# Logits in eight 64x32 tiles over two banks, spaced gathers and another order of the end: an image kernel on one Trainium2 core

## The reference, cut to what matters

```
x = x + conv_ref(ln_c(x))              # LayerNorm over channels, GroupNorm in 8 groups,
                                       # 1x1 conv, relu, 1x1 conv
t = to_tokens(x)                       # 16384 tokens of 64 values per image
t = t + ffn_ref(ln_t(t))

def ffn_ref(x):                        # 32 experts, each takes its 8 best tokens
    logits = einsum('bsd,ed->bse', x, gate_w) + gate_b
    probs  = softmax(logits, axis=1)   # over the tokens of an image
    vals, idx = top_k(probs.transpose(0, 2, 1), 8)
    gathered = take_along_axis(x, flat_idx)
    pooled = einsum('bked,bke->bed', gathered, vals)
    h = gelu([pooled, 1] @ weight1[e]) # 64 -> 256
    out = [h, 1] @ weight2[e]          # 256 -> 64
    outputs.at[flat_idx].add(out * vals)
```

## Time and profile before

| what | value |
|---|---|
| three runs | 659.89, 661.95, 662.16 us, median 661.95 |
| profiled execution | 660.21 us, its span 658.5 us |
| PE busy | 546.5 us, 83% |
| DVE busy | 488.9 us, 74% |
| ACT busy | 429.1 us, 65% |
| POOL busy | 186.4 us, 28% |
| images in the middle | 65.0 us each |
| last image and end | from 502.75 us on |

### The profile page before, as it was taken

The page is one execution under the profiler, slowest core; times in us unless marked ns, Lnnn a source line. Parts: engine busy times, 40 slices in busy tenths (PEclk is TensorE's granted clock), DMA queues, the critical chain, the costliest instruction groups (busy, mean ns, idle before and its releaser), DMA issues.

```text
span 658.5 us, 14319 instructions
## 1 busy us (share of the span) xinstructions
PE 546.5 (83%) x5838; PEld 278.4 (42%) x5838; DVE 488.9 (74%) x955; ACT 429.1 (65%) x603; POOL 186.4 (28%) x110
## 2 busy tenths in 40 slices
PE   3669989998989898989898989898879849768693
PEld 1234444443444344444444444344434314247563
DVE  5575565889788978897889789978886838697501
ACT  2454778678967896888688867887788525543110
POOL 1008252207120712070208020802070540010612
PEclk9856999999999999999999999999989968796555
DMA  8950246533644364436444543454112524310000
GB/s 197 198 122 26 80 135 171 137 112 109 172 122 121 109 179 108 127 113 177 113 114 119 170 128 100 127 162 128 42 58 99 166 83 129 102 65 1 20 10 8
DMA packets 26753, 73.40 MB, mean 111 GB/s; under 512 B 4152, under 2 KB 4152, under 8 KB 22592
## 3 DMA queue, kind: packets, MB, share of 16 engines
q1 hardware_dynamic: 25664, 71.44, 39.5%
q0 software_dynamic: 1024, 1.05, 0.6%
HBM read 38.40 MB, written 34.08 MB: 110 GB/s over the span
## 4 chain that ended last, share of the span: by engine, by line
PE 41%; DVE 29%; ACT 13%; issue 12%; another core or an unknown queue 2%; DMA 2%; POOL 0%; SPq 0%; ACTq 0%; POOLq 0%; DVEq 0%
PE st L364 10%; ACT junk L737 7%; DVE xs L878 6%; PE cv L375 6%; PE tl L392 5%; PE cv L383 5%; PE bc L485 5%; DVE us L868 5%; DVE lg L866 3%; DVE top_i L965 2%; ACT tok L702 2%; DVE us L870 2%; DVE cnd L960 2%; ACT hid L697 2%
## 5 line engine op out<-in xcount | busy, mean ns | idle before, releaser
L1283 POOL TENSOR_TENSOR xs<-xs,us 128x1024 f32<-128x1024 f32 x64 | 151.1, 2376 | 365.9 <-DVE xs L878 173.1
L878 DVE SCALAR_TENSOR_TENSOR xs<-cv,vecs,xs 128x1024 f32<-128x1024 f32 x64 | 82.1, 1282 | 59.5 <-PE cv L383 49.0
L697 ACT ACTIVATE hid<-cv,b1n 128x1024 f32<-128x1024 f32 x64 | 71.2, 1113 | 42.5 <-PE cv L375 42.1
L730 ACT ACTIVATE sqc<-us 128x1024 f32<-128x1024 f32 x64 | 67.5, 1055 | 44.0 <-DVE us L868 43.3
L868 DVE TENSOR_TENSOR us<-xs,bc 128x1024 f32<-128x1024 f32 x60 | 72.9, 1216 | 19.2 <-PE bc L485 18.8
L392 PEld LDWEIGHTS tl<-ident,xs 128*128 128x128 f32 x512 | 63.8, 195 | 54.6 <-issue 54.4
L485 PE MATMUL bc<-rstd_s,spread 32*128 32x256 f32 x368 | 48.4, 340 | 41.3 <-DVE gsum L870 20.3
L364 PE MATMUL st<-xs,stat_w 128*32 128x256 f32 x1024 | 73.7, 409 | 10.6 <-DMA xs<-in_x 9.0
L737 ACT ACTIVATE junk<-us 128x1024 bf16<-128x1024 f32 x64 | 67.3, 1051 | 22.8 <-DVE gsum L870 22.1
L870 DVE CUSTOM_DVE_ANT_0 us<-us,bc 128x1024 f32<-128x1024 f32 x60 | 72.9, 1215 | 11.2 <-PE bc L485 10.0
L401 PE MATMUL tl<-xs,gcen 128*32 128x256 f32 x1024 | 71.6, 390 | 7.8 <-ACT tok L702 6.8
(11 more groups left out here) (184 smaller groups left out, 654.4 us busy)
## 6 DMA issues: line engine op xcount, KB each, us to landing
xs<-in_x SPq DMA_DIRECT2D x64, 512.0 KB, 6.9
out_rows<-tok SPq DMA_DIRECT2D x64, 512.0 KB
us<-in_e_w SPq DMA_DIRECT2D x8, 260.0 KB
xs<-in_e_w SPq DMA_DIRECT2D x8, 256.0 KB
sqc<-out_rows,idx_all POOLq DMA_INDIRECT x16
out_rows<-sqc,idx_all POOLq DMA_INDIRECT x16, 2.1
vecs<-in_b SPq DMA_DIRECT2D x4, 0.2 KB, 13.7
gate_bias<-in_gate_b SPq DMA_DIRECT2D x4, 0.1 KB, 12.1
```

Source lines behind the costliest of these rows:

```text
L697: nc.scalar.activation(hid[:], cv[:], ACT.Relu, bias=b1n[:, par:par + 1]).then_inc(h_done, 1)
L878: nc.vector.scalar_tensor_tensor(out=xu, in0=cv[:], scalar=vecs[:, 3:4], in1=xu, op0=ALU.add, op1=ALU.add).then_inc(x1_done, 1)
L1283: nc.gpsimd.tensor_tensor(xu, xu, su, ALU.add).then_inc(s_done, 1)
```

## The change

1. `logits` uses eight tiles of 64 input rows by 32 output columns. The two halves of the pixels go to two banks, `lgp` and `pt`, 256 columns in each, so the zero half of the weights is no longer multiplied. `logits_copy` reads 256 columns of both banks.
2. The L and E spreads use four products of 64x128 from a new constant `spread2`, which VectorE builds at the start by 32 small operations. The scaling takes a whole piece of 1024 contiguous columns and needs two units of logits and no others; `top_values` waits for its own piece only.
3. The ring has 5 pieces in place of 6; buffers that lay in the sixth are put elsewhere.
4. `candidates` has two more operations on 128x32, since the places inside a piece are laid out otherwise.
5. The token norm of images 0 to 5 runs in steps 5, 6 and 7, and its ScalarE part one step later.
6. Before gathers 0 to 5 GpSimd waits for the last image's x1 of 2, 3 and 4 units and its relu of 4, 5 and 6 units, in turn.
7. In the end, M comes right behind `experts_turn(0)`, all top-8 work stands ahead of VectorE's copies of the turn, and `add_rows` is split: the first half stands ahead of pass 1's `experts_in`, the second behind its `experts_up`. Pass 1's token norm stands ahead of the first `result_rows` and `equal_pixels(3)`.

```diff
-RING = 6
+RING = 5
-DIAGS_AT, PAIR_AT, NORM_AT = (1, 2, 3), (2, 4, 5), (4, 5, 6)
+DIAGS_AT, PAIR_AT, NORM_AT = (1, 2, 3), (2, 4, 5), (5, 6, 7)
...
-        h_banks, add_banks = (st1[:], pt, pd, pc), (st1[:], pc)
+        h_banks, add_banks = (st1[:], pt, pd, pc), (lgp, st2[:])
...
-                            c, col = 2 * sub + h, UN * u + CH * sl + SUB * sub
-                            mm = pe.matmul(lgp[NE * c:NE * c + NE, SUB * sl:SUB * sl + SUB], gcen[:, NE * h:NE * h + NE],
-                                           xs[par][:, col:col + SUB], start=True, stop=True)
+                            c, col, r = 2 * sl + sub, UN * u + CH * sl + SUB * sub, slice(C * h, C * h + C)
+                            mm = pe.matmul(lg_banks[h][NE * c:NE * c + NE, 0:SUB], gcen[r, NE * h:NE * h + NE],
+                                           xs[par][r, col:col + SUB], start=True, stop=True)
...
+                if kind in ("L", "E"):
+                    for h in range(2):
+                        for w in range(2):
+                            r, col = slice(C * w, C * w + C), P * (2 * k + h)
+                            mm = pe.matmul(bc[:, CH * w + SUB * h:CH * w + SUB * h + SUB], spread2[r, col:col + P], rstd2_s[r, :],
+                                           start=True, stop=True)
...
-                    dve.wait_ge(lcopy_done, NU * t + u + 3)
-                    lt = lg[:, place(t, u // 2):place(t, u // 2) + 2 * PIECE]
-                    lt = lt.rearrange("p (i w sl r) -> p w i sl r", i=2, w=2, sl=2)[:, u % 2]
-                    ins = nc.vector.tensor_tensor(lt, lt, bc_l, ALU.mult)
+                    dve.wait_ge(lcopy_done, NU * t + 2 * k + 2)
+                    ins = nc.vector.tensor_tensor(piece(t, k), piece(t, k), bc[:], ALU.mult)
...
+                link(nc.vector.tensor_scalar(top_hi[:], top_i[:], SUB, None, ALU.bitwise_and))
+                link(nc.vector.scalar_tensor_tensor(out=pix, in0=top_hi[:], scalar=float(HW // SUB - 1), in1=pix,
+                                                    op0=ALU.mult, op1=ALU.add))
...
+            for q in range(4):
+                r = slice(32 * q, 32 * q + 32)
+                for k in range(PIECES):
...
+                    nc.vector.tensor_copy(both[:, q % 2], picked)
+                    nc.vector.tensor_scalar(both[:, 1 - q % 2], picked, 0.0, None, ALU.mult)
...
             for b in range(6):
+
+                pool.wait_ge((x1_done, h_done)[b % 2], NU * (NB - 1) + 2 + (b + 1) // 2 + b % 2)
                 gather(b)
```

More of the change, by code:

```diff
@@ L189, in mk_metaformer_kernel @@
         eq = xs[0][:, HW // 2:HW].rearrange("p (b f i) -> p b f i", b=NB, f=GATHERS)
-        late = lg[:, 2 * PIECE:4 * PIECE]
+        late = lg[:, 2 * PIECE:3 * PIECE]
         pool_f = late[0:C + 1, 0:NE * NB + 3 * NB]
-        zsq = [eq[:, 6:8].rearrange("p b f i -> p (b f i)"), late[:, CH:2 * CH]]
-        diags = [eq[:, 7 - p % 2].rearrange("p f i -> p (f i)") for p in range(3)] + [late[:, 2 * CH:3 * CH]]
+        zsq = [eq[:, 6:8].rearrange("p b f i -> p (b f i)"), sqx[:, 0:CH]]
+        diags = [eq[:, 7 - p % 2].rearrange("p f i -> p (f i)") for p in range(3)] + [late[:, CH:2 * CH]]
         hg = us[1][:, 0:4 * CH]
@@ L475, in spread_stat @@
                     return
+                if kind in ("L", "E"):
[4 more added lines that the diff above has]
+                                           start=True, stop=True)
+                    mm.then_inc(bc_filled, 1)
+                    return
                 for i in range(2):
                     for sl in range(2):
[L478 to L484, removed]
+                        c, w = 2 * (k % 2) + sl, 2 * C * (2 * (k // 2) + i)
+                        weights, stat = spread[32 * c:32 * c + 32, w:w + 2 * C], mean_s if kind == "C" else rstd_s
                         mm = pe.matmul(out[:, CH * sl + SUB * i:CH * sl + SUB * i + SUB], weights,
@@ L602, in experts_up @@
                     pe.wait_ge(ebias_ready, 1)
-                    pe.wait_ge(tok_done, NU * NB)
-                else:
-                    pe.wait_ge(row_ready, 2)
+                    pe.wait_ge(lcopy_done, NU * NB)
                 for e in range(NE):
@@ L638, in expert_rows, with add_rows @@
                 mm.then_inc(ob_done, 1)
[L640 to L651, removed]
+            def add_rows(i):
+                pe.wait_ge(z_done, i // 2 + 1)
+                pe.wait_ge(eq_ready, 3 + i // 2)
+                if i < 2:
+                    pe.wait_ge(lcopy_done, NU * NB)
+                else:
+                    pe.wait_ge(row_ready, i - 1)
+                for b in range(*ADDS[i]):
+                    for g in range(GATHERS):
+                        col = GATHERS * C * (b - ADDS[i][0]) + C * g
+                        for f in range(GATHERS):
+                            mm = pe.matmul(add_banks[i % 2][:, col:col + C], eq[:, b, f, P * g:P * g + P], zc[:, b, f, :],
+                                           start=(f == 0), stop=(f == GATHERS - 1))
+                mm.then_inc(add_done, 1)
             tokens(NB - 1, 1, NU - 1)
@@ L675, in _ @@
             expert_rows(1)
-            add_rows(1)
+            for i in (2, 3):
+                add_rows(i)
         @block.scalar
@@ L711, in logits_copy @@
                 col = place(b, u // 2) + CH * (u % 2)
[L712 removed]
+                nc.scalar.activation(lg[:, col:col + CH].rearrange("p (h r) -> p h r", h=2),
+                                     tl[:].rearrange("p (h r) -> p h r", h=2)[:, :, 0:SUB], ACT.Copy).then_inc(lcopy_done, 1)
             def square_x1(b, par, u):
@@ L957, in top_values @@
                 link = Steps(dve, top_steps, TOP_STEPS * t + 2 * i)
-                for k in range(2 * (i // 2), 2 * (i // 2) + 2):
-                    dve.wait_ge(bc_used, scaled(t, k))
+                dve.wait_ge(bc_used, scaled(t, i))
                 link(nc.vector.max(cnd[:, K * i:K * i + K], piece(t, i)))
@@ L1218, in _ @@
             use_spread(NB, "E", 3)
-            lns(nc.vector.tensor_tensor(id2[:], ident[:, 0:C], ident[:, C:P], ALU.add))
-            top_values(7, 2)
-            top_places(7, 2)
-            turned(0)
-            top_values(7, 3)
-            top_places(7, 3)
-            expert_outs(0)
-            candidates(7)
-            contributions(0)
+            for i in (2, 3):
+                top_values(7, i)
+                top_places(7, i)
+            turned(0)
+            candidates(7)
+            lns(nc.vector.tensor_tensor(id2[:], ident[:, 0:C], ident[:, C:P], ALU.add))
             use_spread(NB, "M", NB - 1)
@@ L1230, in _ @@
             merge_values(NB - 1, link)
+            expert_outs(0)
             diagonals(3)
-            for i in (0, 1):
-                result_rows(i)
-            equal_pixels(3)
+            contributions(0)
             token_norm(1, 6, NB)
             pooled(1)
+            result_rows(0)
+            result_rows(1)
+            equal_pixels(3)
             turned(1)
```

18 lines of the change are left out of this document (10 added, 8 removed).

## The result

The changed kernel takes 679.88 us in the median of four runs (678.69 to 682.41), the kernel before 661.16 (659.89 to 662.16). The ratio is 1.0296, with a 95% interval from 1.0268 to 1.0324: 3% slower, where a gain of 1.4% was forecast. The profiled execution has a span of 676.9 us, against 658.5.

A forecast was written before the change was run, and what follows sets the result against it. No engine is full (PE 83%); a ring of waits bounds the kernel. 660.2 − 8.0 − 0.7 + 0.3 + 0.1 + 0 = 651.9 us; as the profiled execution lies 1.7 under its median, forecast 652.8, range 645 to 661.

The forecast's parts named there:

- part on the logits: Logits: about 0.4 us gained a unit, hidden beside VectorE's scaling except in the first image; −0.7 us, bounds nothing to −3.0.
- (d): Less streaming in every step makes TensorE's clock fall; six falls cost 14.4 us, giving 666 us, slower; chance 0.12.
- The 2.4: Images: the cost in us of one clock fall, from an image of 67.45 us against 65.00.
- (c): PE is the bound after all: shorter logits give 626 us, in a weak form 645 to 649; chance 0.10.
- Gathers: Last image: gathers spaced in groups of 2, 4, 4 and 2 shorten VectorE's wait; −8.0 us, bounds −3.7 to −12.9.
- 12.9 less four lags: Last image: hole and cold PE cost 12.9 us; four groups each leave 1.2, so 4.9 remain and 8.0 go.
- Token norm: Last image: eighth unit's x1 3.6 us earlier, 3.7 given back behind the merge; +0.1 us, from −1 to +2.
- End order: End: PE's last product of pass 0 starts 5.2 us later, offset by covered waits; 0, bounds ±4.
- Start, candidates, spreads, ring: Start: 32 small operations cost +0.3 us, from 0 to +1.7; candidates, spreads and the ring of five: nothing.

The follow-up runs named there:

- 128-row run: Changed kernel with logits again as 128x32 tiles with half-zero weights, all else of the change kept: 657.17 us, ratio 0.9955 to the kernel before.
- doubled one: Changed kernel with each of its 64x32 logits products computed twice into the same place: 662.71 us, ratio 1.0048 to the kernel before.
- Spacing alone: Kernel before plus only the waits ahead of gathers 0 to 5: 655.73 us, ratio 0.9933.
- late scatters: Changed kernel with 128-row logits, useless products in the end, and GpSimd's second six scatters held until experts_down(1) is done: 649.69 us, ratio 0.9844.

## Why the prediction was wrong

**The clock, and the step that failed.** The failing step is in the part on the logits: "Bounds: nothing, and 0.35 for each image with the first twice, −3.0". Work of 26 us was taken off TensorE and its price bounded by nothing from below. The loss was put among the rivals (d) with a chance of 0.12, "TensorE's clock falls in images where it now stays at 1.00", and against it stood "PE stays busy 55 of 65 us". That was the wrong reason. With the new logits it is busy for 57.45 of 66.04 us and falls all the same. In place of the term of −0.7, with 0 as its upper bound, the images lost 19.8 us. Rival (d) is what happened. That its 14.4 for six falls is near to that is in part luck, for two errors go against each other: there were 12 falls more than before, not six, and each cost some 1.7 us, not 2.4. The 2.4 was read from windows that are not cut at x1. From x1 to x1 the image of before with the fall is only 1.4 longer than the one ahead of it:

```profile
442.87:509.50 66.63, 57.99 (x630) 28.15 (x634) 54.48 (x101) 51.01 (x72) 18.91 (x8) 0.97 0.24 79
377.66:442.87 65.21, 58.52 (x664) 28.64 (x666) 56.35 (x104) 51.76 (x73) 18.95 (x8) 1.00 0.47 130
```

The first image alone lost 2.3, the fourth 4.8. The 128-row run puts the loss at 22.7 us in the medians, and the doubled one brings 17.2 of it back. With 128-row logits and all else of the change the kernel takes 657.17, which lies in the forecast's range: this one term carried it out.

The Trainium skill, "TensorE: Matmul & The Clock Gate", HAM oscillation, describes a kernel in which short compute between waits for DMA lets the clock fall again and again, and advises to restructure the loop so that TensorE stays busy. The runs agree in the direction, though TensorE waits here for VectorE and not for DMA, and for 1.60 us in the rows above: more useless work gave 17.2 us back.

**Logits on the path.** That they are off it in the images of the middle was right, and rival (c) is out. In image 5 the distances from x1 to x1 are 9.01, 8.45, 10.08, 9.37, 9.89, 7.60 and 7.55 us in the changed kernel, and 9.01, 8.53, 8.55, 9.37, 7.60, 7.60 and 7.54 before. The two that are longer, by 1.5 and 2.3, are those with a fall in them; in the others the shorter logits bring at most 0.1. The block's own time was right too: 0.66, where half the time and 0.1 for the change of tile shape had been put together. The 0.7 in the first image cannot be seen beside the two falls there. (The bound of −3.0 is 9 times 0.35, so 3.15.)

**Gathers.** The mechanism was right, and the size is in part luck. Spacing alone gained 7.3 in the last image, where I said 8.0. But this is not 12.9 less four lags: at the hole, from the third x1 to the fifth, 10.0 us came back, and 2.4 were lost where the token norm waits for the rows, which the sum did not have. In the changed kernel the groups are 2, 4, 4 and 2, VectorE's idle times at these x1 are 0.69 and 0.74, and two waits of ScalarE are called remote, together 5.5. With the moved norm the last image gained 12.8, and 13.3 in the changed kernel. But the gain counts only if the end stays as long, and it did not: the same end takes 83.86 at a clock of 0.64 and 89.41 at 0.58. Alone the change is worth 4.5 us in the medians. I had priced the clock only beside the gathers, where it was to rise, and took the end's clock as given.

**Token norm.** Forecast: 3.6 earlier at the eighth x1, 3.7 given back, +0.1. Measured: 5.5 and 5.1. The sum was right, the parts were not: beside the 3.3 of ScalarE's wait the move also took away the wait for gathered rows, 3.1, which there is only when the gathers are spaced.

**End order.** Forecast: 0, between −4 and +4. With the clock about equal (0.62 and 0.59), it is +0.8 in the medians (657.2 against 656.4) and 1.8 in the profiled executions: right. In the changed kernel the end lost 12.9 in all, of which 4.0 until the first top-8 of image 7 (the norm), 3.4 more until the last scaling (`experts_up(0)` at half clock, 7.1 in place of 4.1), 5.1 until `experts_down(0)` starts (the 5.2 that I had), 3.4 and 4.7 in the two `experts_down`. What came back is 6.8 between them (I had 5.7 and M's 1.0) and 0.9 in the turn. These are rows of the chain of the changed kernel:

```profile
614.31 1.24 PE bc L471 x2
615.55 7.65 PE cv L627 x128
```

So the second step that failed is the end's 0 with its bounds of ±4: I let the clock only stay or rise there. It fell, and `experts_down(0)` took 7.65, 6.93 of it busy at a clock of 0.50, in place of 4.21. And the sum had no price for the scatters that now lie beside `experts_down(1)`.

**Start, candidates, spreads, ring.** Nothing, as forecast, within what can be seen. The first x1 comes at 54.49 in the changed kernel, 55.47 before, and at 54.4 to 56.2 in the experiments, with no order by whether the 32 operations are in; +0.3 cannot be told from that.

What stays open: what, beyond the work in a step, decides in which image the clock falls; and how much a shorter filler would bring in either end.

## What to carry to other kernels

Before work is taken off TensorE, ask first whether a wait behind it ends with it. If not, nothing is gained, and the emptier steps may cost the clock: here 26 us less work cost 20. Price the clock in each stretch on both sides, also in stretches whose code does not change. Where TensorE must wait in a long serial end, products without use in the wait can pay (7.4 us in the new end), but what the clock gives back must outweigh the time by which they are longer than the wait: in the old end it did not. Let no row of indirect DMAs fall on a chain of short instructions, and when gathers are spaced, look at who needs their rows.

## What the runs showed of the hardware

- TensorE's granted clock fell when 26 us of its work were spread thin over 64 units: images 1 to 6 had it busy for 57 to 62 of 66 to 70 us (0.84 to 0.89) at a mean clock of 0.90 to 0.97. With the long logits it was busy for 58.6 of 65.2 us (0.90) at 1.00, and with the short ones twice for 59.3 of 65.6 at 1.00. The busy times at a lower clock contain products that took up to twice as long.
- A fall that lies on the chain cost 1.4 us (the doubled run, 67.02 against 65.61) to 2.3 us (image 5 of the changed kernel).
- The 128 entries of `experts_down`, each a 128x64 weight load and an 8-column product, take 3.93 us at a clock of 1.00 (late scatters), 4.21 at a mean of 0.91 (before) and 7.03 at 0.50 (spacing alone). The loads alone are busy for 3.81, 4.09 and 6.91 us: they scale with the clock too.
- While twelve indirect DMAs were issued in a row, VectorE's x1 came 10.32 us late for a wait that no engine of the core explains; with groups of two and four the distance of these two x1 fell from 16.57 to 7.30 us. That the DMAs held up the signals of the other engines is inferred from this. Indirect DMAs beside the 8-column products opened holes of 1.1 us in TensorE's instruction stream, with no wait to be seen; without them the block ran in one piece of 3.93.
- The same end of a program took 83.86 us at a clock of 0.64 and 89.41 at 0.58. The ten runs of spacing alone go the same way: the five over 656 us have a mean clock of 0.903 to 0.908, the five under 655 one of 0.910 to 0.919.
